# Fourth layer of a four-layer graph network: the sum over eight heads moves from GpSimd to one VectorE operation

## What is computed

```python
q = (atom_embeddings @ Wq + bq).reshape(b, m, h, d)
...
scores = jnp.einsum('bmhd,bnhd->bhmn', q, k) * scale
scores = scores + jnp.transpose(edge_bias[edges], (0, 3, 1, 2))
scores = jax.nn.leaky_relu(scores, NEG_SLOPE)
...
attn = jax.nn.softmax(scores, axis=-1)
out = jnp.einsum('bhmn,bnhd->bmhd', attn, v).reshape(b, m, h * d)
return out @ Wp + bp
...
x = _layernorm(x + _L3_gnn_ref(...), axis=-1)
```

## Time and profile before

| | |
|---|---|
| median of 3 runs | 5131.23 us (5131.02 to 5134.22) |
| the profiled execution | 5130.21 us |
| its span, first to last instruction | 5128.3 us |
| granted clock of TensorE, mean | 0.981 of full speed |
| VectorE busy | 4852.0 us, 95% of the span |
| ScalarE busy | 4776.8 us, 93% |
| TensorE busy | 4605.9 us, 90% |
| GpSimd busy | 3782.0 us, 74% |

### The profile page before, as it was taken

The page is one execution under the profiler, slowest core; times in us unless marked ns, Lnnn a source line. Parts: engine busy times, 40 slices in busy tenths (PEclk is TensorE's granted clock), DMA queues, the critical chain, the costliest instruction groups (busy, mean ns, idle before and its releaser), DMA issues. The chain is left out here.

```text
span 5128.3 us, 118848 instructions
## 1 busy us (share of the span) xinstructions
PE 4605.9 (90%) x48920; PEld 1816.5 (35%) x48920; DVE 4852.0 (95%) x5715; ACT 4776.8 (93%) x5793; POOL 3782.0 (74%) x3450
## 2 busy tenths in 40 slices
PE   7888888888888989999899998997889999999998
PEld 2222222222222223232222323234445555555554
DVE  7999999999999999999999999996779999999998
ACT  7999999999999999999999999996879999999997
POOL 8999999999999999999999999993303223222333
PEclk9999999999999999999999999998879999999999
DMA  1010000000000000000000000004410011010100
GB/s 53 32 32 31 27 32 32 26 32 32 32 26 32 18 11 9 11 12 12 9 12 11 10 11 11 12 9 134 138 24 18 24 24 24 16 24 24 24 16 13
DMA packets 154142, 138.53 MB, mean 27 GB/s; under 512 B 53318, under 2 KB 120646, under 8 KB 153606
## 3 DMA queue, kind: packets, MB, share of 16 engines
q1 hardware_dynamic: 152902, 130.87, 8.9%
q10 hardware_dynamic: 704, 0.07, 0.0%
HBM read 103.64 MB, written 18.87 MB: 24 GB/s over the span
## 5 line engine op out<-in xcount | busy, mean ns | idle before, releaser
L200 POOL TENSOR_SCALAR a_hid_p<-a_BLOS,a_PHI,a_PLO 128x1024 f32<-128x1024 f32 x2688 | 3152.7, 1192 | 153.0 <-PE apsS L326 145.6
L450 DVE SCALAR_TENSOR_TENSOR a_hid_p<-apsB,a_THI,a_hid_p 128x1024 f32<-128x1024 f32 x2560 | 3078.0, 1277 | 15.9 <-POOL a_hid_p L200 14.0
L326 PE MATMUL apsS<-a_hid_p,a_sel_high 128*32 128x512 f32 x10752 | 2645.3, 599 | 190.1 <-ACT a_hid_a L365 119.8
L326 PE MATMUL apsS<-a_hid_a,a_sel_high 128*32 128x512 f32 x6144 | 1923.2, 598 | 48.6 <-ACT a_hid_a L365 27.8
L326 PE MATMUL apsS<-a_hid_a,a_sel_low 128*32 128x512 f32 x5632 | 1684.7, 598 | 96.3 <-DVE a_hid_p L450 53.6
L365 ACT ACTIVATE a_hid_a<-a_BHI,a_ALH 128x1024 f32<-128x1024 f32 x1536 | 1690.1, 1142 | 0.0
L365 ACT ACTIVATE a_hid_a<-a_BLO,a_ALH 128x1024 f32<-128x1024 f32 x1408 | 1566.7, 1141 | 0.0
L326 PEld LDWEIGHTS apsS<-a_hid_p,a_sel_high 128*32 128x32 f32 x10752 | 584.5, 109 | 962.1 <-issue 545.7
L752 PE MATMUL m3S<-xT,Q 64*128 64x512 f32 x2048 | 594.9, 655 | 28.1 <-ACT x_even L796 14.3
L326 PEld LDWEIGHTS apsS<-a_hid_a,a_sel_high 128*32 128x32 f32 x6144 | 419.5, 109 | 562.6 <-issue 299.1
L326 PEld LDWEIGHTS apsS<-a_hid_a,a_sel_low 128*32 128x32 f32 x5632 | 376.1, 109 | 638.2 <-DVE a_hid_p L450 334.1
(11 more groups left out here) (183 smaller groups left out, 3906.5 us busy)
## 6 DMA issues: line engine op xcount, KB each, us to landing
a_adj_in<-adj SPq DMA_DIRECT2D x64, 512.0 KB, 3.8
adj_in<-adj SPq DMA_DIRECT2D x64, 512.0 KB, 4.6
mask_rows<-a_mask SPq DMA_DIRECT2D x64, 256.0 KB, 2.2
a_mask<-mask_rows SPq DMA_DIRECT2D x64, 256.0 KB, 2.6
mask<-mask_rows SPq DMA_DIRECT2D x64, 256.0 KB, 2.8
Xr<-x_odd SPq DMA_DIRECT2D x128, 64.0 KB, 2.1
out<-yn SPq DMA_DIRECT2D x64, 32.0 KB, 1.5
x_even<-x SPq DMA_DIRECT2D x1, 256.0 KB, 2.8
```

Of the source, the lines that this page charges most:

```text
L200: gp.tensor_scalar(hid_p[:, at % RING_P, :], BLOS[:, g % 2, :], PHI[:, g % 2, m:m + 1], PLO[:, g % 2, m:m + 1], ALU.min, ALU.max).then_inc ...
L326: last = pe.matmul(psS[32 * q:32 * q + 32, h * HALF:(h + 1) * HALF], sel[:, 28 - 4 * p:60 - 4 * p], unit, start=s == 0 and layer == 0, sto ...
L450: dve.scalar_tensor_tensor(out=hid_p[:, at % RING_P, :], in0=psB[:, :], scalar=THI[:, g % 2, m:m + 1], in1=hid_p[:, at % RING_P, :], op0=A ...
```

## The change

GpSimd's three additions over the heads are gone. Behind the scaled product, VectorE now waits for that product to be written (`aux_out`) and for GpSimd to have read the previous sum (`summed`), and reduces `prod` over the heads in one `tensor_reduce` whose input is viewed with the head as the innermost index: neighbouring inputs lie 64 floats, 256 bytes, apart, and there are 64 outputs of 8 inputs each. GpSimd waits for the new semaphore `head_sum` and adds the row and x, as before.

```diff
@@ -617,8 +617,8 @@
         scored, leaky_ready, min_ready, probs_ready, turned, weighed, o_out = (
             sem("scored"), sem("leaky_ready"), sem("min_ready"), sem("probs_ready"), sem("turned"), sem("weighed"), sem("o_out"))
         aux_made, aux_out = sem("aux_made"), sem("aux_out")
-        inverted, halved, summed, y_ready, stats_ready, var_ready, eps_added, rstd_ready, normed = (
-            sem("inverted"), sem("halved"), sem("summed"), sem("y_ready"), sem("stats_ready"), sem("var_ready"),
+        inverted, head_sum, summed, y_ready, stats_ready, var_ready, eps_added, rstd_ready, normed = (
+            sem("inverted"), sem("head_sum"), sem("summed"), sem("y_ready"), sem("stats_ready"), sem("var_ready"),
             sem("eps_added"), sem("rstd_ready"), sem("normed"))
         stored = [sem(f"stored{i}") for i in range(2)]
         block = ctx.enter_context(nc.Block())
@@ -681,17 +681,11 @@
 
         @block.gpsimd
         def _(gp):
-            def add_heads(m):
-                gp.wait_ge(aux_out, done("project", *divmod(m, tiles)))
-                gp.tensor_tensor(part[:, 0:4 * C], prod[:, 0:4 * C], prod[:, 4 * C:8 * C], ALU.add).then_inc(halved, 1)
-                gp.wait_ge(halved, 3 * m + 1)
-                gp.tensor_tensor(part[:, 4 * C:6 * C], part[:, 0:2 * C], part[:, 2 * C:4 * C], ALU.add).then_inc(halved, 1)
-                gp.wait_ge(halved, 3 * m + 2)
-                gp.tensor_tensor(part[:, 6 * C:7 * C], part[:, 4 * C:5 * C], part[:, 5 * C:6 * C], ALU.add).then_inc(halved, 1)
-                gp.wait_ge(halved, 3 * m + 3)
-                gp.tensor_tensor(part[:, 7 * C:8 * C], part[:, 6 * C:7 * C], w["row"], ALU.add).then_inc(summed, 1)
+            def add_rows(m):
+                gp.wait_ge(head_sum, m + 1)
+                gp.tensor_tensor(part[:, C:2 * C], part[:, 0:C], w["row"], ALU.add).then_inc(summed, 1)
                 gp.wait_ge(summed, m + 1)
-                gp.tensor_tensor(y[:, m % 2, :], part[:, 7 * C:8 * C], X[:, m * C:(m + 1) * C], ALU.add).then_inc(y_ready, 1)
+                gp.tensor_tensor(y[:, m % 2, :], part[:, C:2 * C], X[:, m * C:(m + 1) * C], ALU.add).then_inc(y_ready, 1)
 
             def normalise(m):
                 gp.wait_ge(var_ready, m + 1)
@@ -706,7 +700,7 @@
                                  ALU.mult).then_inc(normed, 1)
 
             for m in range(T):
-                add_heads(m)
+                add_rows(m)
                 normalise(m)
 
         @block.tensor
@@ -864,13 +858,16 @@
                 else:
                     m = b * tiles + i
                     dve.wait_ge(probs_ready, HEADS * (m + 1))
-                    if m >= 1:
-                        dve.wait_ge(halved, 3 * m - 2)
                     dve.reciprocal(rden, den[:, m % 8, :]).then_inc(inverted, 1)
                     dve.wait_ge(inverted, m + 1)
                     dve.tensor_tensor(prod.rearrange("p (h c) -> p h c", c=C), psA.rearrange("p (h c) -> p h c", c=C),
                                       rden.rearrange("p (h o) -> p h o", o=1).to_broadcast([P, HEADS, C]),
                                       ALU.mult).then_inc(aux_out, 1)
+                    dve.wait_ge(aux_out, done(*job))
+                    if m >= 1:
+                        dve.wait_ge(summed, m)
+                    dve.tensor_reduce(part[:, 0:C], prod.rearrange("p (h c) -> p c h", c=C), mybir.AxisListType.X,
+                                      ALU.add).then_inc(head_sum, 1)
 
             def deviations(m):
                 dve.wait_ge(y_ready, m + 1)
```

## The result

The changed kernel takes **5173.58 us** (median of 4 runs, 5168.10 to 5174.90) where the kernel before took 5132.02 (5131.02 to 5134.22) beside it. The ratio is 1.0078, with a 95% interval of 1.0065 to 1.0091: slower by 0.8%, 41.6 us. The forecast was 5147.5 us, slower, with a range of 5138 to 5184.

What follows compares the result with a forecast made beforehand. VectorE's queue was taken to bound the fourth layer: 0.11 + 0.61 - 0.54 + 0.13 = +0.31 us per tile, times 61 is +18.9, less 2.6 behind the loop, giving 5147.5 us; range 5138 to 5184.

Steps and rivals of the forecast that it cites:

- (a): VectorE's reduction must wait until the scaled product is written: +0.11 us per tile.
- (b): The reduction itself in VectorE's queue, 512 float32 in and 64 out: +0.61 us per tile, bounds 0.34 and 1.14.
- the tail: Behind the loop, the last two tiles' head-sum chain gets shorter: -2.6 us in all.
- The strided rival: Reduction inputs 256 bytes apart cost double: reduction 1.14 us, tile +0.84, total 5180.8 us; chance 24%.
- (c): The second minimum's stall under GpSimd's 256-element addition goes: -0.54 us per tile.
- (d): GpSimd's remaining 64-element row addition holds the second minimum: +0.13 us per tile, bounds 0 and 0.54.
- the minimum would go first: Rival: the second minimum passes GpSimd's row addition, no stall remains; tile +0.18, total 5139.6 us; chance 11%.
- Two elements at a time: Rival: VectorE's reduction reads in pairs, costing 0.34 us; tile +0.04, total 5130.7 us, not slower; chance 4%.
- The sum: Per-tile terms total +0.31 us over 61 tiles, +18.9, less 2.6 behind the loop: +16.3 us.

Runs made afterwards that it cites:

- heads in pairs: Changed kernel, same result, with the two heads of a pair stored as neighbours for each channel in `prod`: 5152.17 us, ratio to before 1.0045.
- the kernel with heads side by side: Changed kernel, same result, with the product written so that a channel's eight heads are neighbours in `prod`: 5179.39 us, ratio to before 1.0086.
- the moved changed kernel: Changed kernel with VectorE's reciprocal, product and reduction moved behind the two minima of their pair step: 5174.62 us, ratio to before 1.0075.
- the moved kernel: Kernel before the change with VectorE's reciprocal and scaled product moved behind the two minima of their pair step: 5113.85 us, ratio 0.9955.
- the last kernel: Kernel before the change, projection behind the minima, and GpSimd adding the constant row to x before it waits for the product: 5099.15 us, ratio 0.9940.

## Why the prediction held in sign and missed in size

- **VectorE is the bound, and a microsecond in its queue is one in the tile**: right. 0.65 per tile in the queue, 0.65 in the tile, here; 0.31 and 0.31 (20.85 to 20.86 between query copies) with heads in pairs. Five variants of the reduction, heads in pairs among them, and three of GpSimd's additions moved the layer by 61 times their step within 3 us; the kernel with heads side by side came 3.5 us above it, and the moved changed kernel fell 6 short of the 8 expected, 4 of them in the tiles at a graph's end.
- **(a), the wait for the product**, +0.11: right to the hundredth, 0.72 between the starts.
- **(b), the reduction**, +0.61: this is the step that failed. It measured 0.95. The shape was right (dense, the record is 0.686 as in the earlier trace rows, and the cost to the queue 0.60); the distance between inputs was set at nothing. 61 x 0.34 is 20.7 of the 26 us by which the forecast was short; the tail is 1.5 more. I had let TensorE's matmul with a 16-byte step weigh more than the rule on lines; it does not carry over to VectorE, whose own runs show an edge between 8 and 16 bytes.
- **The strided rival** had the mechanism and overpriced it: 1.14 for 0.95, 5180.8 for 5173.6. The time came out 26 us above the forecast and outside its likeliest span of 5141 to 5157, and 7 us below the rival. The range held because it had been stretched to take in the rival, not because the forecast was near.
- **(c) and (d), the stalls**, -0.54 and +0.13: right in both, and the price by GpSimd's elements, 2.08 ns each, held at three lengths. That the minimum would go first, as under L705, was wrong: L686 wins in every tile.
- **Two elements at a time**: wrong, 0.686 us for 512.
- **The tail**, -2.6 by the forecast, -1.6 with the slow rival. From product to statistics of the last but one tile:

```profile
5150.25 0.16 DVE L861 RECIPROCAL rden<-den 128x8 f32<-128x8 f32 x1
...
5162.35 0.69 DVE L863 TENSOR_TENSOR prod<-m3A,rden 128x512 f32<-128x512 f32 x1
...
5164.94 0.23 DVE L878 BATCH_NORM_STATS2 stats<-y 128x6 f32<-128x64 f32 x1 [0.83 <-POOL y L688]
```

2.59 us against 3.25, 0.66 less, which is the forecast's working with 1.03 in place of 0.69. From the reciprocal at 5150.25 to the end it is 22.86 us, 23.96 before: -1.1. The forecast's working with the measured reduction gives -1.9, and from the last but one product to the last row addition it was 2.1 less (5.09 against 7.15 us); but from GpSimd's last scaling to the end the profile after took 2.73 us where the one before took 1.93. In the other profiles this last stretch, which holds the store of the result, took 1.93 or 2.70 to 3.00 us; what sets it was not looked into.
- **The sum** with the measured reduction: 61 x 0.65 - 1.1 = 38.6, against the layer's 39.7. That leaves 1.9 of the 41.6 between medians. It is not assigned: ahead of the layer, where nothing was changed, executions differ by several microseconds, and why they do was not looked into.

## What to carry to other kernels

On an engine that has no idle time left, taking work over from an idle one costs its full price, and even a helper whose stalls cost the busy engine half a microsecond per tile was cheaper than doing its job. Before moving such work, look at which of the busy engine's instructions the helper's run beside: shorter pieces, or a place beside transposes, cut the stall to half or less and gained 0.25% to 0.6% where the move lost 0.8%. A view with an innermost step of 16 or 256 bytes cost a float32 reduction of VectorE 1.65 to 1.7 times its time per element, and a write with a step of 32 bytes some 1.75 times; storing pairs side by side avoided it on both sides.

## What the runs showed of the hardware

- VectorE, float32: steps of 4 and 8 bytes run at 0.686 us for 512 inputs, steps of 16 and 256 bytes at 1.064 and 1.032. The larger step is slightly the faster. A product that writes with a step of 32 bytes takes 1.087 instead of 0.692; with a step of 8 bytes it takes 0.694.
- The number of outputs of a reduction, 64 or 256, changes nothing: 0.686 us.
- A minimum waits for GpSimd's elements only, 0.54, 0.26 and 0.13 us for additions of 256, 128 and 64, and not for the fixed part of the addition, so not for the whole of GpSimd's instruction.
- Which of the two goes first when a first minimum ends is not settled by which came first. In the moved kernel GpSimd's addition of x began 0.03 us after the first minimum, at 4789.78, and went ahead of the second; the scaling L705 began 0.06 after one, at 4791.81, and was passed. It is so throughout: in the kernel before, the scaling began 0.05 to 0.10 us into a first minimum in 37 of 64 tiles and lasted 2.6 us in each; in the others it began at least 0.27 us before one, or after the last, and took 0.58 to 0.59. The early addition of the last kernel began 0.00 to 0.29 us into one in 20 tiles and went ahead of the second in each. The addition reads two tensors and the scaling one and two columns of scalars; whether that is the reason was not tried.
